# The short scan of a cross-attention and FFN kernel, from TensorE to four shifted additions on VectorE

## What is computed

```python
h = rmsnorm(layernorm(x), g_res) @ W_in.T + b_in           # 512 x 512
u = exp(-EPSILON) * rmsnorm(ctx, g_init)[:, :512]           # 512 x 512
s[n] = u[n] + a * s[n - 1]                                  # scan over rows, a = exp(-dt), about 0.001
x = x + h + s[plug]        # plug: the patch of each position, from patch_lens
y = layernorm(x)
y_prev = y shifted by one position
r = sigmoid((mu_r * y + (1 - mu_r) * y_prev) @ W_r.T)
k = relu((mu_k * y + (1 - mu_k) * y_prev) @ W_k.T) ** 2
x = x + r * (k @ W_v.T)
```

## Time and profile before

| | |
|---|---|
| median of 3 runs | 786.25 us (785.98 to 786.61) |
| profiled execution | 788.05 us, span 786.5 us |
| PE busy | 756.9 us (96%) |
| PE weight loads | 624.1 us (79%) |
| VectorE (DVE) busy | 553.8 us (70%) |
| ScalarE (ACT) busy | 413.3 us (53%) |
| GpSimd (POOL) busy | 173.4 us (22%) |
| TensorE clock granted | 0.986 of full speed over the span |

### The profile page before, as it was taken

The page is one execution under the profiler, slowest core; times in us unless marked ns, Lnnn a source line. Parts: engine busy times, 40 slices in busy tenths (PEclk is TensorE's granted clock), DMA queues, the critical chain, the costliest instruction groups (busy, mean ns, idle before and its releaser), DMA issues.

```text
span 786.5 us, 11081 instructions
## 1 busy us (share of the span) xinstructions
PE 756.9 (96%) x3462; PEld 624.1 (79%) x3463; DVE 553.8 (70%) x1005; ACT 413.3 (53%) x681; POOL 173.4 (22%) x175
## 2 busy tenths in 40 slices
PE   7669899999999999999999999999999999999997
PEld 4457688888888888888888888888888888888876
DVE  4678797685866868586686858667685867667452
ACT  3317755454654645466464546656454665544760
POOL 7244131311213131121313112131311213130000
PEclk9879999999999999999999999999999999999999
DMA  7476153441706244170624417062441706231011
GB/s 256 150 188 166 60 124 132 112 143 47 209 2 167 88 110 144 46 208 0 156 98 109 144 43 211 0 166 88 108 146 41 212 0 160 94 102 20 1 54 54
DMA packets 42765, 85.73 MB, mean 109 GB/s; under 512 B 3536, under 2 KB 3536, under 8 KB 42704
## 3 DMA queue, kind: packets, MB, share of 16 engines
q1 hardware_dynamic: 30624, 63.71, 21.7%
q0 software_dynamic: 9216, 16.78, 13.5%
q10 hardware_dynamic: 2880, 4.76, 1.7%
HBM read 64.26 MB, written 21.76 MB: 109 GB/s over the span
## 4 chain that ended last, share of the span: by engine, by line
PE 85%; DVE 4%; POOL 4%; issue 2%; ACT 2%; DMA 1%; DVEq 0%; POOLq 0%; ACTq 0%
PE bank L484 27%; PE bank L486 27%; PE bank L485 27%; PE bank L588 3%; POOL ring L426 2%; DMA s_rows<-scanned 1%; POOL decay L363 1%; DVE xk_lo L894 1%; DVE scratch L989 0%; DVE ring L1019 0%; DVE gate L1044 0%; ACT scratch L794 0%; POOL rs_a L389 0%; DVE bn_a L923 0%; DVE bn_b L1025 0%
## 5 line engine op out<-in xcount | busy, mean ns | idle before, releaser
L426 POOL DMA_INDIRECT ring<-s_rows,patch_now x60 | 99.4, 1656 | 245.8 <-DMA s_rows<-scanned 214.6
L894 DVE TENSOR_TENSOR xr_lo<-scratch,xr_hi 128x512 fp32r<-128x512 f32 x124 | 85.6, 690 | 68.9 <-ACT xr_hi L704 68.4
L989 DVE SCALAR_TENSOR_TENSOR scratch<-turned,cols,scratch 128x512 f32<-128x512 f32 x128 | 94.6, 749 | 34.4 <-ACT scratch L749 15.0
L484 PE MATMUL bank<-wi_hi,xt_hi 128*128 128x512 f32 x256 | 104.0, 406 | 5.1 <-DVE xt_lo L894 5.1
L704 ACT ACTIVATE turned<-bank 128x512 f32<-128x512 f32 x64 | 33.4, 604 | 143.3 <-PE bank L588 114.7
L484 PE MATMUL bank<-xk_hi,wk_hi 128*128 128x512 f32 x256 | 99.9, 390 | 2.2 <-DVE xk_lo L894 2.2
L485 PE MATMUL bank<-wi_lo,xt_hi 128*128 128x512 f32 x256 | 101.8, 398 | 0.0
L486 PE MATMUL bank<-wi_hi,xt_lo 128*128 128x512 f32 x256 | 101.5, 396 | 0.0
L484 PE MATMUL bank<-wr_hi,xr_hi 128*128 128x512 f32 x256 | 99.7, 389 | 0.8 <-DVE xr_lo L894 0.8
L486 PE MATMUL bank<-xk_hi,wk_lo 128*128 128x512 f32 x256 | 99.6, 389 | 0.0
L485 PE MATMUL bank<-xk_lo,wk_hi 128*128 128x512 f32 x256 | 99.6, 389 | 0.0
(11 more groups left out here) (131 smaller groups left out, 1283.5 us busy)
## 6 DMA issues: line engine op xcount, KB each, us to landing
ring<-in_x SPq DMA_DIRECT2D x16, 1024.0 KB, 7.4
out<-gate SPq DMA_DIRECT2D x64, 256.0 KB
xt<-in_x_turned SPq DMA_DIRECT2D x15, 1024.0 KB, 5.2
ctx_rows<-in_ctx SPq DMA_DIRECT2D x16, 512.0 KB, 8.0
s_rows<-scanned ACTq DMA_DIRECT2D x16, 256.0 KB, 2.0
gate<-in_L_xattn_W_in SPq DMA_DIRECT2D x4, 256.0 KB, 3.4
xt<-in_x_turned SPq DMA_DIRECT2D x2, 512.0 KB, 6.3
turned<-in_L_ffn_W_r SPq DMA_DIRECT2D x1, 1024.0 KB, 7.8
```

The source lines that it names most:

```text
L426: pool.indirect_dma_start(ring[b.slot][:, t, :], None, s_rows[:, :], bass.IndirectOffsetOnAxis(ap=rows, axis=0), compute_op=ALU.add).then_ ...
L484: nc.tensor.matmul(where, lhs_hi, rhs_hi, start=start, stop=False)
L894: return nc.vector.tensor_tensor(to, whole, high, ALU.subtract)
L989: nc.vector.scalar_tensor_tensor(scratch[:, 2 + i % 2, :], turned[:, c, 1:S + 1], cols[:, 1 + which, c:c + 1], scratch[:, i % 2, :], ALU.m ...
```

## The change

From batch 2 on (every `new` of iterations 0 to 13) the scan is made of four steps with k = 8, 4, 2, 1: `earlier` gets the rows moved down by k, then `scanned = a^k * earlier + before`. Each move is one transfer from SBUF to SBUF of 120, 124, 126 and 127 rows of 2 KB, issued by GpSimd; VectorE does the four additions and a fifth for the bias. The head of `earlier` is zeroed once per batch. u_hi, u_lo and the product of PE are gone but for batches 0 and 1, and PE no longer waits for `s_copied` ahead of tile 3; its wait for `far_over` stays. `scan_input` moves ahead of `ka_low(b, 0)`. ctx is loaded first, then x, then xt. In the far branch VectorE now makes u_hi and u_lo itself.

```diff
 # SyncE, iteration(b)
+                    reached(sp, far_over, new.plus(-1), 1, 1)
                     rows_added(sp, new.plus(-1))
-                    reached(sp, xt_lo_ready, new.plus(-1), 2, 2)
-                    load_xt(new)
-
+                    load_ctx(new)
                     reached(sp, out_ready, b.plus(-1), T, T)
                     ...
                     load_x(new)
-                    reached(sp, far_over, new.plus(-1), 1, 1)
-                    load_ctx(new)
+                    reached(sp, xt_lo_ready, new.plus(-1), 2, 2)
+                    load_xt(new)
 # GpSimd
+            def shift_scan(b):
+                since = b.plus(-2)
+                for n, (k, _) in enumerate(steps_of_scan):
+                    if n == 0:
+                        reached(pool, u_ready, b, 1, 1)
+                    else:
+                        reached(pool, earlier_added, since, STEPS, n)
+                    hold(pool, pool_passed)
+                    of = scanned if n else u
+                    pool.dma_start(earlier[k:P, :], of[0:P - k, :]).then_inc(earlier_loaded, 16)
@@ iteration(b): behind root_a(new), root_c(new) (in iteration 0 root_c, root_a)
                 if new.exists(B):
+                    if not is_first(new, 1):
+                        shift_scan(new)
                     far(new)
                     add_patches(new)
 # TensorE, turn(b) and iteration(b)
                     if t == SCAN and b.plus(1).exists(B) and not is_first(b):
-                        reached(pe, s_copied, b.plus(1), 1, 1)
                         reached(pe, far_over, b.plus(1), 1, 1)
...
                 if new.exists(B):
-                    scan(new)
                     far(new)
 # ScalarE: u_high(new) gone (twice)
 # VectorE
+            def scan_step(b, n):
+                since = b.plus(-2)
+                reached(dve, earlier_loaded, since, 16 * STEPS, 16 * (n + 1))
+                ...
+                nc.vector.scalar_tensor_tensor(scanned[:, :], earlier[:, :], steps_of_scan[n][1], (scanned if n else u)[:, :],
+                                               ALU.mult, ALU.add).then_inc(earlier_added, 1)
+            def add_bias(b):
+                reached(dve, earlier_added, b.plus(-2), STEPS, STEPS)
+                nc.vector.tensor_tensor(scanned[:, :], scanned[:, :], bias[:, :], ALU.add).then_inc(s_copied, 1)
@@ iteration 0
+                    clear_head(new)
                     ka_low(b, 0)
                     ...
                     ka_low(b, 3)
-                    u_low(new)
+                    scan_step(new, 0)
                     norm_b(nxt)
                     gating(b, 0)
                     gating(b, 1)
+                    scan_step(new, 1)
                     x_lo(new, 0)
                     x_lo(new, 1)
-                    scan_out(new)
+                    scan_step(new, 2)
+                    add_out(b, 0)
+                    add_out(b, 1)
+                    scan_step(new, 3)
+                    add_bias(new)
                     far(new)
                     dve.sem_inc(far_over, 1)
-                    add_out(b, 0)
-                    add_out(b, 1)
@@ later iterations
+                    clear_head(new)
                     stats_a(new)
                     stats_c(new)
                 if nxt.exists(B):
                     norm_b(nxt)
+                if new.exists(B):
+                    scan_input(new)
                 for m in range(C):
                     if b.exists(B):
                         ka_low(b, m)
                     if new.exists(B):
                         if m in (1, 2):
                             x_lo(new, m - 1)
-                        if m == 2:
-                            scan_input(new)
+                        if m in (2, 3):
+                            scan_step(new, m - 2)
...
-                if new.exists(B):
-                    u_low(new)
                 if b.exists(B):
                     gating(b, 0)
                     gating(b, 1)
                 if new.exists(B):
-                    scan_out(new)
+                    scan_step(new, 2)
+                if b.exists(B):
+                    add_out(b, 0)
+                    add_out(b, 1)
+                if new.exists(B):
+                    scan_step(new, 3)
+                    add_bias(new)
                     far(new)
                     dve.sem_inc(far_over, 1)
                 if b.exists(B):
-                    add_out(b, 0)
-                    add_out(b, 1)
                     gating(b, 2)
                     gating(b, 3)
```

More of the change, by code:

```diff
@@ L71, in batches, with shift_steps @@
         iteration(Batch(0, n))
+def shift_steps(powers):
+    return [(k, powers[k] if k < len(powers) else 0.0) for k in (8, 4, 2, 1)]
 def decay_powers():
@@ L96, in build @@
     powers = decay_powers()
+    steps_of_scan = shift_steps(powers)
+    STEPS = len(steps_of_scan)
+    assert len(powers) <= 2 ** STEPS
     input_gain = math.exp(-EPSILON)
@@ L162, in build @@
         patch_now = sb("patch_now", [P, T], U32)
+        earlier = sb("earlier", [P, D])
         def part(row, start, shape, dt):
@@ L520, in far @@
                         else:
-                            reached(pe, s_copied, b, 1, 1)
+                            if b.fixed and b.number() < 2:
+                                reached(pe, s_copied, b, 1, 1)
+                            pe.wait_ge(far_u_lo, n[1] * T + 1)
                         product(scan_bank(b)[:, :], decay_hi[:, 1, :], decay_lo[:, 1, :], u_hi[:, :], u_lo[:, :],
                                 True, False).then_inc(far_carried, 1)
-                        pe.wait_ge(far_u_lo, done)
+                        pe.wait_ge(far_u_lo, n[1] * T + c + 1)
                         product(scan_bank(b)[:, :], decay_hi[:, 0, :], decay_lo[:, 0, :], u_hi[:, :], u_lo[:, :],
@@ L829, in iteration @@
                     squares(b)
-                    u_high(new)
                 if new.exists(B) and not is_first(new, 1):
@@ L845, in iteration @@
                 elif new.exists(B):
-                    if not is_first(b):
-                        u_high(new)
                     store_scan(new)
@@ L945, in scan_input, with clear_head @@
                 reached(dve, rs_c_done, b, 1, 1)
-                reached(dve, u_lo_ready, b.plus(-1), 1, 1)
+                if b.fixed and b.number() < 3:
+                    reached(dve, u_lo_ready, b.plus(-1), 1, 1)
+                else:
+                    reached(dve, earlier_added, b.plus(-3), STEPS, STEPS)
                 nc.vector.scalar_tensor_tensor(u[:, :], ctx_rows[:, 0:D], rs_c[:, :], g_ctx[:, :],
                                                ALU.mult, ALU.mult).then_inc(u_ready, 1)
+            def clear_head(b):
+                reached(dve, earlier_added, b.plus(-2), STEPS, 0)
+                nc.vector.memset(earlier[0:steps_of_scan[0][0], :], 0.0).then_inc(head_zeroed, 1)
+            def scan_step(b, n):
+                since = b.plus(-2)
+                reached(dve, earlier_loaded, since, 16 * STEPS, 16 * (n + 1))
+                if n == 0:
+                    reached(dve, head_zeroed, since, 1, 1)
+                    reached(dve, s_stored, b, 16, 0)
+                    reached(dve, u_ready, b, 1, 1)
+                else:
+                    reached(dve, earlier_added, since, STEPS, n)
+                nc.vector.scalar_tensor_tensor(scanned[:, :], earlier[:, :], steps_of_scan[n][1], (scanned if n else u)[:, :],
[3 more added lines that the diff above has]
+                nc.vector.tensor_tensor(scanned[:, :], scanned[:, :], bias[:, :], ALU.add).then_inc(s_copied, 1)
             def far(b):
@@ L953, in far @@
                 with dve.If(n[0] > 0):
+                    if b.fixed and b.number() < 2:
+                        reached(dve, s_done, b, 1, 1)
+                    nc.vector.tensor_copy(u_hi[:, :], u[:, :]).then_inc(far_u_hi, 1)
+                    dve.wait_ge(far_u_hi, n[1] * T + 1)
+                    low(u_lo[:, :], u[:, :], f32(u_hi[:, :])).then_inc(far_u_lo, 1)
+                    dve.wait_ge(far_u_lo, n[1] * T + 1)
                     for c in range(1, T):
@@ L973, in far @@
                         nc.vector.tensor_copy(u_hi[:, :], u[:, :]).then_inc(far_u_hi, 1)
-                        dve.wait_ge(far_u_hi, done)
+                        dve.wait_ge(far_u_hi, n[1] * T + c + 1)
                         low(u_lo[:, :], u[:, :], f32(u_hi[:, :])).then_inc(far_u_lo, 1)
```

1 line of the change is left out of this document (added).

## The result

The kernel after takes 871.62 us in the median of four runs (871.29 to 872.65), the kernel before 786.43 us beside it: 1.1086 times as long, 95% interval 1.1067 to 1.1105. The profiled execution took 871.79 us, its span 870.2 against 786.5, so 83.7 us are to be found in the two traces; the medians are 85.2 apart.

What follows compares the result with a forecast made beforehand. PE's own work was taken to bound the kernel; a chain of three transfers would make it wait: 40.3 (13 periods) + 10.0 (iteration 0) + 10 (clock) = +60, 846 us on the median, range 799 to 903.

Steps and rivals of the forecast that it cites:

- the forecast's own case: L between 2.2 and 4.1 us, total time 799 to 903 us; chance 0.70.
- L: Time from a DVE step's end to the next step's start, through one GpSimd transfer: 3.2 us taken, 2.15 to 4.1 estimated.
- the clock: TensorE's granted clock falls after PE's new wait: five falls taken, +10 us; bounds none or 14 x 2 = 28 us.
- The removed matmuls: Three scan matmuls a batch gone from PE, 0.68 us per iteration; hidden in PE's idle time, so worth nothing.
- The place of the chain: PE's wait for far_over before the turn's last four transposes is the one with least room: slack 4.2 us.
- The fixed part: Period from projection to projection without its three transfers: 39.48 us, giving 39.48 + 3L.
- Iteration 0: Its first step waits behind GpSimd's root_a, so the next projection starts at 114.8 against 104.73: +10.0 us.
- Loads: SyncE's loads start later, about 12.6 us behind the projection's start; no cost, 1.9 us of cover for xt.
- a chain beyond L = 4.1: Rival: transfers take L of 4.1 to 5 us, through stores or slower POOL; 903 up to 960 us; chance 0.10.
- the few engines: Rival: shifts use few DMA engines, 127 rows on one, 124 on four; 1010 us; chance 0.10.
- the faster case: Rival: L under 2.16 us as SBUF answers sooner than DRAM, PE's floor holds; 783 us; chance 0.06.
- 811: Total in us, without the clock term, using the Trainium skill's estimated 2.6 us per GpSimd transfer in place of L.

Runs made afterwards that it cites:

- e3: Kernel after with two scan steps only (k = 2 and 1; shifts by 8 and 4 left out): 782.52 us, ratio 0.9939.
- e8: Kernel after with three scan steps (k = 4, 2 and 1; shift by 8 left out): 800.71 us, ratio 1.018.
- e7: Kernel after with add_out of tiles 0 and 1, and so their stores, moved behind far_over: 863.96 us, ratio 1.0966.
- e5: Kernel after with the same four shift transfers issued by SyncE in place of GpSimd: 1030.76 us, ratio 1.309.
- e9: Kernel after with steps k = 2 and 1; in iteration 0 the first shift precedes root_a, add_bias and far_over precede x_lo: 778.14 us, ratio 0.9886.
- e4: Kernel after with 16 useless matmuls on PE ahead of its wait for far_over in each turn: 852.61 us, ratio 1.0829.
- e6: Kernel before with only SyncE's load order changed to ctx, x, xt: 787.1 us against 786.96, ratio 1.0004.
- e2: Kernel after without PE's wait for far_over in the turn, and with ScalarE's store_scan moved behind turned_out: 826.35 us, ratio 1.0494.

## Why the prediction was right, and where its terms were off

The sum said +60 us, 846; measured were +85, 872, inside the range of 799 to 903 and in the forecast's own case. The mechanism is the predicted one: PE waits for `far_over` behind three transfers, and e3, e8, e7 and e5 move the loss by making this chain shorter or longer. The size is off by 25 us, nearly all in L and the clock. By its steps:

- **The bound.** PE's period of 45.97 and its floor of 45.29 hold: e3 and e9 run at 45.28 to 45.32.
- **The removed matmuls** are worth nothing in after, and 0.68 a turn as soon as the chain is short enough (e9). Shown.
- **The place of the chain.** PE waits ahead of tile 3 for `far_over`, in every turn. The slack of 4.2 us fits all three: with one link it isn't used up (e3), with two it is just about used up (e8), with three it is exceeded.
- **L.** This is the term that was mis-sized most. 3.2 was taken, 3.61, 3.34 and 3.92 measured, 10.87 in place of 9.6 in an iteration: 13 x 1.27 = +16.5 us. In the middle link the errors nearly cancel, which is luck: GpSimd's instruction was taken too long (0.95 for 0.54), dispatch too short by 0.1, and what follows the instruction too short, 1.72 for 2.23. The DMA view above says where: the 0.56 us ahead of the packets and the 0.5 behind them are together the 1.05 that was called completion, but the packets take 1.2 us and not 0.67. q0 has 13696 - 9216 = 4480 packets more than before, 80 for a transfer, and 18.4% x 16 x 870.2 - 13.5% x 16 x 786.5 = 863 us for them, 0.19 each, where 9 at 0.074 to an engine were taken from the store on q10. The last link has 0.56 more from the output stores (e7), 13 x 0.56 = 7 of the 16.5: "some tenths, inside the bounds of L" was right as a bound and not put into the sum.
- **The clock.** Five falls at 2 us were taken, +10. It fell in all 14 turns. Thirteen falls lie in the periods, at 1.5 each: 19 us by e4. The fourteenth is the 1.9 us behind the last turn: 84.2 us are left there in before, e3, e8 and e9, where the clock stayed up, and 85.8 in e4, where the last wait of 2.31 us made it fall. The step that failed in it is "the new wait of 3.8 us is shorter than both [4.43 and 6.40]", from which a count between none and 14 was guessed. PE's waits came out at 3.67 to 4.65, 4.15 in the mean without the last of 6.26, so the row of 4.43 was the nearest, and it had said a fall. A still shorter pair stood in the trace of before and was not looked at, in its timeline of PE and its stretches:

```profile
24.97 0.47 PE L484 MATMUL bank<-u_hi,decay_hi 128*128 128x512 f32 x1 [2.08 <-DVE u_lo L894]
...
26.62 0.78 PE L484 MATMUL bank<-wi_hi,xt_hi 128*128 128x512 f32 x1 [0.71 <-DVE xt_lo L894]
```

```profile
28.00:30.00 2.00, 2.00 (x6) 1.56 (x5) 2.00 (x4) 0.08 (x1) 0.00 (x0) 0.50 0.84 294
```

Waits of 2.08 and 0.71 us close together, and the clock at 0.50 behind them: this row, too, spoke for a count near 14.
- **The fixed part** of the period, 39.48, came out as 51.52 - 10.87 - 1.48 = 39.17: steps of 0.69 and not 0.75, a bias addition with its wait of 0.73 and not 0.84, at the tail 1.77 for 1.72. 13 x -0.31 = -4.
- **Iteration 0:** +11.2 for +10.0, by the distance from `v_b`. The +9.7 between the two traces looks better than it is by 1.6 us of earlier start.
- **Loads.** ctx, x and xt in the new order cost nothing (e6). They start 12.1 to 13.7 us behind the projection's start, for 12.6 predicted. With their later start, 4.9 us of VectorE's time in all lie in waits for x. e2 shows the limit behind: there xt is the wait.

Together 60.3 (40.3 + 10.0 + 10) + 16.5 + 9.2 - 4.0 + 1.9 + 1.2 = 85.1, of the 85.2 between the medians.

The rivals: a chain beyond L = 4.1 didn't come; the few engines are real on SyncE's queue (e5) and not on GpSimd's, where 127 rows take no longer than 126 (e7); the faster case needed L under 2.16, and even the shortest link is 3.34. The Trainium skill's fit (DMA: Bandwidth & Descriptors, section Anatomy of one DMA), an estimate of 2.6 us, stands beside 2.7 and 2.8 to landing for the two shifts that meet no store. For a link from engine to engine 0.6 us of dispatch comes on top. At the prediction's 4.3 us for each 0.1 us of L this is 26 of the 61 us by which 811 was too low; the stores beside the last link and the clock, which that sum left out, are most of the rest.

Open: why the first link of a batch takes 3.5 where the second takes 3.34, with 124 rows in after and e7 and with 127 in e9. Open too: what decides a fall of the clock behind a short wait. In e7 a wait of 3.55 us brought none, where 3.46 and 3.50 did, and that one period was 49.08 in place of some 51.

## What to carry to other kernels

A step that is free by volume (VectorE idled 30%) is not free as a chain: count how many hand-overs by DMA lie one behind the other, take each from the end of the writer to the start of the reader (here 3.35 to 3.9 us), and hold their sum against the slack of the one wait that is nearest on the bound engine. Before adding steps, ask what the last ones contribute: with an a of about 0.001 two steps do here what four do, and turn +11% into -0.6%, and into -1.1% with iteration 0 put right. And where the bound engine starts to wait, price what follows the wait as well, by the rows of the waits nearest in length.

## What was not expected of the hardware

- The granted clock of TensorE fell behind the wait of each of after's 14 turns, 3.67 us and more, and behind none of the single waits of 0.2 to 1.0 us in the turns of e4. Waits of 3.46 to 3.81 in e7 made it fall too, but for one; so did 2.31 us in the last turn of e4. In e3 two waits of 1.80 and 1.48 us, with four transposes between them, were enough. The length of one wait does not settle it: in iteration 0 of e9 the waits at 86.6, 88.4 and 90.2 are 0.34, 0.79 and 0.85 us, and the clock fell to 0.5 at 90.2; in before the three waits at the same place are 0.36, 0.78 and 0.85, and it stayed at 1.00.
- Direct transfers of GpSimd between SBUF and SBUF used 80 packets for 120 to 127 rows of 2 KB, fewer than there are rows, and spread evenly enough that 124, 126 and 127 rows take the same 3.4 to 3.5 us. On SyncE's queue the same transfers took 5.6, 3.1 and 13.1 us.
- GpSimd's instruction for a direct transfer took 0.53 us in the median for the three links (0.88 at most) and 0.65 for the first shift; an indirect one took 1.55 to 2.09.
- Two stores of 256 KB that meet a transfer of 254 KB cost it 0.56 us.
